# One more score product at the head of each step of the row maxima

## The reference

```python
x = conv(x)                        # Mamba layer: selective scan over 1024 tokens, 16 states a channel,
                                   # group norm, SiLU, residual
t = tokens(x)
t = t + attention(layer_norm(t))   # 8 heads of 8 channels, causal
t = t + experts(layer_norm(t))     # 8 experts, the 2 best of each token
```

```python
att = jnp.einsum('bqhd,bkhd->bhqk', q, k) * scale
att = jnp.where(causal, att, -jnp.inf)
att = jax.nn.softmax(att, axis=-1)
```

## Time and profile before

| what | value |
|---|---|
| median of 3 runs | 1633.64 us (1631.91 to 1634.67) |
| the profiled execution | 1626.1 us, span 1624.0 us |
| PE busy | 1260.7 us, 78% |
| DVE busy | 1171.9 us, 72% |
| ACT busy | 704.3 us, 43% |
| POOL busy | 512.2 us, 32% |
| mean granted clock of PE | 0.761 |

### The profile page before, as it was taken

The page is one execution under the profiler, slowest core; times in us unless marked ns, Lnnn a source line. Parts: engine busy times, 40 slices in busy tenths (PEclk is TensorE's granted clock), DMA queues, the critical chain, the costliest instruction groups (busy, mean ns, idle before and its releaser), DMA issues. The chain is left out here.

```text
span 1624.0 us, 17597 instructions
## 1 busy us (share of the span) xinstructions
PE 1260.7 (78%) x6388; PEld 499.9 (31%) x6388; DVE 1171.9 (72%) x1388; ACT 704.3 (43%) x1298; POOL 512.2 (32%) x272
## 2 busy tenths in 40 slices
PE   2455346888888987888887987888888988899894
PEld 1111111323233333333333323333233324433433
DVE  3396398787678968887679867887688867348345
ACT  1423322347434762376335642476326631460470
POOL 2454454344334332342243333342144321000000
PEclk9567556659966998589867997599758985695696
DMA  1100320021202111201211120201220120020000
GB/s 38 45 1 13 83 53 13 7 68 30 55 8 68 30 32 38 67 1 30 62 29 45 30 50 19 68 10 23 47 61 14 30 49 17 19 51 21 3 14 7
DMA packets 25863, 54.87 MB, mean 34 GB/s; under 512 B 8531, under 2 KB 8919, under 8 KB 23448
## 3 DMA queue, kind: packets, MB, share of 16 engines
q1 hardware_dynamic: 25776, 53.73, 14.6%
HBM read 28.15 MB, written 12.98 MB: 25 GB/s over the span
## 5 line engine op out<-in xcount | busy, mean ns | idle before, releaser
L926 DVE TENSOR_REDUCE row_max<-ps 128x1 f32<-128x768 f32 (+7 forms) x384 | 355.9, 952 | 142.2 <-PE ps L1202 139.6
L660 POOL TENSOR_TENSOR read<-state,c_rep 128x1024 f32<-128x1024 f32 x128 | 303.9, 2374 | 466.2 <-DVE state L970 450.6
L801 ACT ACTIVATE probs<-ps 128x512 f32<-128x512 f32 (+3 forms) x768 | 329.5, 496 | 144.7 <-PE ps L1305 86.5
L970 DVE TENSOR_TENSOR_SCAN state<-decay,drive 128x1024 f32<-128x1024 f32 x128 | 357.1, 2790 | 1.8 <-POOL read L660 1.1
L1198 PE MATMUL ps<-k_stack,q_stack 72*128 72x512 bf16 (+3 forms) x768 | 280.6, 456 | 83.2 <-DVE row_max L926 64.3
L1302 PE MATMUL ps<-q_stack,k_stack 75*128 75x512 bf16 (+3 forms) x768 | 222.8, 353 | 32.7 <-DVE drive L979 17.8
L979 DVE TENSOR_TENSOR drive<-ps,b_rep 128x512 f32<-128x512 f32 x256 | 169.6, 676 | 105.7 <-PE ps L1236 105.0
L762 ACT ACTIVATE decay<-ps,a_scale 128x512 f32<-128x512 f32 x256 | 175.3, 696 | 116.8 <-DVE state L970 100.1
L1236 PE MATMUL ps<-dt_rows,pick 96*128 96x512 bf16 x256 | 120.5, 471 | 96.9 <-DVE drive L979 69.5
L1317 PE MATMUL ps<-probs,v_aug 128*32 128x512 f32 (+3 forms) x1536 | 177.4, 536 | 4.1 <-ACT acc_sb L790 1.6
L1198 PEld LDWEIGHTS ps<-k_stack,q_stack 72*128 72x128 bf16 x768 | 73.8, 116 | 274.2 <-DVE row_max L926 171.4
(11 more groups left out here) (169 smaller groups left out, 1281.6 us busy)
## 6 DMA issues: line engine op xcount, KB each, us to landing
q_stack<-q_parts_dram SPq DMA_DIRECT2D x48, 192.0 KB
k_stack<-k_parts_dram SPq DMA_DIRECT2D x48, 192.0 KB
dt_rows<-read SPq DMA_DIRECT2D x96, 64.0 KB, 2.0
u_rows<-read SPq DMA_DIRECT2D x96, 64.0 KB, 2.0
k_parts_dram<-read SPq DMA_DIRECT2D x40, 128.0 KB, 2.4
q_parts_dram<-read SPq DMA_DIRECT2D x24, 128.0 KB, 2.3
xs<-in_x SPq DMA_DIRECT2D x8, 256.0 KB, 3.5
residual<-in_x SPq DMA_DIRECT2D x8, 256.0 KB, 9.6
```

Of the source, the lines that this page charges most:

```text
L660: pool.tensor_tensor(read[:, k % (2 * NG), :], state[:, k % 2, :], c_rep[:, :], ALU.mult)\
L801: act.activation(probs[:, e % (2 * QUAD), 0:w], bank_of(("scores", e))[:, 0:w], ACT.Exp, scale=SCALE).then_inc(exped.sem, 1)
L926: dve.tensor_reduce(row_max[:, i, h0:h0 + nh], scores[:, :, 0:P * (i + 1)], AX.X, ALU.max, negate=True).then_inc(row_maxed.sem, 1)
L970: dve.tensor_tensor_scan(state[:, k % 2, :], decay[:, k % 2, :], drive[:, k % 3, :], 0.0, ALU.mult, ALU.add).then_inc(scanned.sem, 1)
```

## The change

```diff
+                    def keep_clock(bank, weights, src):
+
+                        pe.matmul(bank, weights, src, start=True, stop=True)
+
...
                         i, h0, nh = SCORE_STEPS[s]
                         if s >= 2:
                             pe.wait_ge(row_maxed.sem, row_maxed.at(b, s - 1))
+                        keep_clock(ps[:, 4 + 2 * (s % 2), :], q_stack[0:9 * DH, h0, tokens(i)],
+                                   k_stack[0:9 * DH, h0, 0:BANK])
                         for hh in range(nh):
                             for h in range(i // QB + 1):
                                 bank = 4 + 2 * (s % 2) + hh + h
```

## The result

The changed kernel took 1663.7 us (median of 3, 1660.4 to 1671.1) against 1633.6 us: 1.019 times as long, 95% interval 1.014 to 1.025. It is slower, by 30 us. The forecast was 59 us slower; what happened lies at the border between its likeliest case and the one called half held.

The account below looks back on a forecast made before the run. PE and DVE were taken as tied in the half-clock score loops. Terms of 56, 9, 0 and -6 us summed to +59 us: 1692 us against the median, range 1665 to 1725 us.

Parts of the forecast that it names:

- its likeliest case: Whole kernel: the forecast itself, 1692 us against the median, range 1665 to 1725 us, chance 0.50.
- half held: Rival: score stages hold the clock in first halves, fall as before in second; 1637 to 1665 us, chance 0.13.
- The price of a product: Score-stage pair loops: 0.43 us per half-clock product, +0.21 us a step; loop 2.89 us; weight load nothing.
- How many steps are at half clock: Eight score stages: 265 steps at half clock, 0.21 us each, 56 us; 119 at full clock, 0.
- the 9 us for steps beside f32 products: Seven stages: some 6 half-clock steps each beside an f32 product pay the other half, 9 us (0 to 18).
- What the extra work gives back by the clock: First 12 steps of three stages: more work may tip the clock up, 12 us at most, -6 us taken.
- Why the clock doesn't rise for most of the stage: Score stages: another kind of work lifts the clock; added 72-row products at half clock only thin it out.
- the mark that I had set for an undersized clock term: Score stages' first halves: shortening by more than 3 us each would show the clock term undersized.
- Held throughout: Rival: added products keep the full clock to the end of each score stage; 1599 us, chance 0.18.
- PE-bound everywhere: Rival: each half-clock score step pays all of 0.43 us, 114 us in sum; 1747 us, chance 0.13.
- Hidden: Rival: DVE's other work and other batches' chains set the stages, hiding products; 1633 us within 3, chance 0.06.
- The stretches between: Seven stretches between the eight score stages: expected unchanged, as the change acts in the stages alone.

Follow-up runs that it names:

- the narrow product: The changed kernel with the added 72-row product cut from 512 to 128 columns, in all steps: 1630.6 us, 0.998 of the kernel before.
- the 128-row run: The changed kernel with the added 512-column product on 128 rows, identity weights, instead of 72 rows, in all steps: 1606.3 us, 0.983 of the kernel before.
- its 72-row control: The changed kernel with identity weights and the 128-row variant's tile and set-up, cut to 72 rows, 512 columns: 1667.4 us, 1.028 of the kernel before.

## Why the prediction was right in sign, and where its size was off

**The price of a product.** Right. 0.43 us at half clock was measured; the widest loop came to 2.91 us (2.89 predicted), and a step in the last stage's second half cost 0.22 us (0.21 predicted). The weight loads cost nothing, as the narrow product shows with all 384 of them.

**How many steps are at half clock, second halves.** Right in size. With their clocks of before (0.50 to 0.62), 24 x (1-k) x 2 gives 181 steps in the second halves and 95 in the first ones (11 more than the 265 of the sum, which came from the means of whole stages). 181 steps at 0.21 us are 38 us, and 38.1 us were measured. Some of that agreement is luck. The grants were forecast at 0.50 to 0.55 there, and only three of the eight were: four rose from 0.52 to 0.57 or more, up to 0.65, one fell from 0.62 to 0.57. And part of the 9 us for steps beside f32 products belongs to these halves too.

**What the extra work gives back by the clock.** This term was mis-sized, and it is the step that failed. I had 12 us at most and took 6. The 95 half-clock steps of the first halves should have cost 20 us, and with their share of the f32 neighbours about 25 (an estimate). Measured: the first halves grew by 0.6 us in sum. So about 24 us came back there, twice my upper bound. I had priced only the first 12 steps of three stages; in fact the grant of the first half rose in seven of the eight stages, in the fourth from 0.77 to 0.96. Two windows of that half, kernel before and kernel after:

```profile
793.40:803.20 9.80, 9.73 (x23) 2.95 (x21) 5.86 (x7) 0.00 (x0) 0.00 (x0) 0.50 0.20 49
```

```profile
800.70:826.40 25.70, 22.17 (x119) 8.37 (x119) 18.95 (x26) 6.21 (x6) 3.78 (x3) 1.00 0.35 77
```

Before, the grant fell some 12.5 us into the stage; after, it stayed at 1.00 for the first 25.7 us. The last stage shows the price without the gift: its grant fell from 0.55 to 0.50, and its first half went from 26.6 to 33.3 us. With 59 - 18 = 41 us, the sum would have stood between the profiled execution's 45 us and the 30 us of the medians.

**Why the clock doesn't rise for most of the stage.** Right for the second halves in the main (0.52 to 0.65 in six stages, 0.50 in the last two), wrong for the first ones. There the argument that more 72-row products only thin out what lifts the clock failed: beside the wide f32 work of other batches they kept it up. That the kind of product decides was an inference from wide 128-row work before the only rise that I showed; the 128-row run and its 72-row control show that the rows do matter, at equal columns.

**Signs that were missed.** DVE's wait for PE grew by 39 us, not 50 or more; the last stage by 12.1 us, not 8, since its first half was PE-bound. Of the first halves only the fourth and sixth shortened by more than 3 us, the mark that I had set for an undersized clock term; the others paid for their products and got much of it back, so the mark was too strict. And the 3 us that I said a measurement can tell is too fine: the three executions of the kernel after lie 10.6 us apart.

**The rivals.** Held throughout: didn't happen, but it is what the 128-row product does, and its price of 1599 us was near (1606.3). That is luck in part: in that run the second halves gave 17 us and the first ones 5, where the rival had 24 and 26 and took 15 off for the products. Half held: close to what happened in the clock, first halves held and second ones not; its time, 1637 to 1665 us, holds the measured 1663.7 at its edge, since it took about 20 us off the second halves' 40, and they paid 38. It had 0.13, too little: the rows of one stage at 1.00 over its first 12 steps spoke for it. PE-bound everywhere: out, a pure step paid 0.22 us; it held in the last stage's first half alone. Hidden: out, DVE's wait grew by 39 us.

**The stretches between** were said to stay as they were; they grew by 6.7 us. Why was not tested; in the 384-column run unchanged code in them took 16 us longer than in the 512-column run on the same chip, at a lower grant, so their own losses of the clock can shift.

## What to carry to other kernels

Work added to keep TensorE's clock up must be priced at both levels. Here it cost nothing that showed where the clock was high and DVE was the bound, and 0.22 us a step, half its 0.43 us, in the pair loops at half clock. The rows that it fills matter: here the same columns at the same places lost 30 us with 72 rows and gained 23 to 26 us with 128. And it pays to try it on parts of the loop: the 72-row product made the kernel 21 us faster when it stood in the first half of each stage alone, and 32 us slower in the second half alone.

## What the runs showed of the hardware that I had not expected

- The granted clock followed the rows a product fills, at equal columns: 0.50 with PE busy 28.7 of 30.2 us (72 rows) and 1.00 with PE busy 17.8 of 23.0 us (128 rows).
- A busy PE doesn't suffice for the full clock: 33.05 of 33.3 us busy with products that are mostly 72 rows high was granted 0.50.
- What is done in one part of the program changes the grant in a later part whose code is the same: second halves of 28.4 to 29.1 us at 0.62 to 0.71 with products in the first halves alone, against 32 at 0.50 to 0.52. In the third stage the full clock came anew after 14 us at half clock, and was not carried over; why it did so in four stages of eight is open.
- The gain need not show in the total: with 128 rows, 384 columns took as long in the stages as 512 (556.0 and 557.0 us) and the kernel 15 us longer (1623.2 and 1607.9 us, same chip), lost in code that doesn't hold the product.
